# Cross attention: the products with V of four key tiles stand together, with eight buffers of probabilities

## The reference

```python
Q = (decoder_input @ W_q).reshape(B, Sd, HEADS, HEAD_DIM)      # B 4, Sd 1024, 16 heads of 32
K = (encoder_output @ W_k).reshape(B, Se, HEADS, HEAD_DIM)     # Se 2048
V = (encoder_output @ W_v).reshape(B, Se, HEADS, HEAD_DIM)
scores = jnp.einsum('bqhd,bkhd->bhqk', Q, K) / jnp.sqrt(jnp.float32(HEAD_DIM))
attn = jax.nn.softmax(scores, axis=-1)
out = jnp.einsum('bhqk,bkhd->bqhd', attn, V).reshape(B, Sd, E)
return out @ W_o + b_o
```

## Time and profile before

| | |
|---|---|
| median of 3 runs | 4630.41 us (4628.96 to 4638.13) |
| profiled execution | 4622.7 us |
| its span | 4621.0 us |
| TensorE (PE) busy | 4050.2 us, 88% |
| VectorE (DVE) busy | 2741.0 us, 59% |
| ScalarE (ACT) busy | 2096.2 us, 45% |
| GpSimd (POOL) busy | 2479.5 us, 54% |

### The profile page before, as it was taken

One profiled execution on the slowest core, in us unless ns is written; L12 is line 12 of the kernel. 1 busy time (PEld: TensorE's weight loads), 2 busy tenths in 40 slices (PEclk: granted clock), 3 DMA queues, 4 the chain that ended last, 5 costly groups with the idle time before them and its releaser, 6 DMA issues. The chain is left out here.

```text
span 4621.0 us, 61708 instructions
## 1 busy us (share of the span) xinstructions
PE 4050.2 (88%) x21906; PEld 2502.5 (54%) x21906; DVE 2741.0 (59%) x4978; ACT 2096.2 (45%) x3869; POOL 2479.5 (54%) x927
## 2 busy tenths in 40 slices
PE   6988999997779997999999999999999663339997
PEld 5874555554568884444444444444444342328885
DVE  4425777773443335777777777777776342316675
ACT  2112555553121110666666666666666322216665
POOL 0001333332000001999999999999999314527887
PEclk8996999998899996999999999999999875559999
DMA  4546454413555555122222222222220366524444
GB/s 146 173 163 127 97 112 95 94 47 128 187 200 171 176 170 135 25 61 64 62 65 56 56 58 56 56 56 56 56 56 6 128 204 97 97 59 74 81 81 64
DMA packets 283077, 449.71 MB, mean 97 GB/s; under 512 B 31384, under 2 KB 131736, under 8 KB 276632
## 3 DMA queue, kind: packets, MB, share of 16 engines
q1 hardware_dynamic: 259064, 407.26, 33.7%
q0 software_dynamic: 19776, 36.85, 4.8%
q10 hardware_dynamic: 3968, 2.10, 0.2%
HBM read 267.22 MB, written 178.91 MB: 97 GB/s over the span
## 5 line engine op out<-in xcount | busy, mean ns | idle before, releaser
L864 DVE TENSOR_REDUCE cross_neg_max<-cross_scores 128x1 f32<-128x512 f32 x2048 | 1265.6, 677 | 414.4 <-PE cross_scores L693 414.4
L653 POOL TENSOR_TENSOR cross_partial<-cross_partial,cross_probs 128x2048 f32<-128x2048 f32 x320 | 1465.6, 4580 | 66.7 <-ACT cross_probs L815 29.6
L815 ACT ACTIVATE cross_probs<-cross_shifted 128x512 f32<-128x512 f32 x2048 | 1074.3, 606 | 762.5 <-PE cross_shifted L705 728.2
L693 PE MATMUL cross_scores<-cross_k_stack,cross_q_stack 96*128 96x512 f32 x2048 | 876.2, 437 | 60.7 <-DMA cross_v<-v 33.1
L705 PE MATMUL cross_shifted<-cross_q_stack,cross_k_stack 98*128 98x512 f32 x2048 | 850.7, 420 | 11.5 <-ACT cross_probs L815 5.6
L705 PEld LDWEIGHTS cross_shifted<-cross_q_stack,cross_k_stack 98*128 98x128 f32 x2048 | 387.2, 190 | 382.7 <-issue 232.9
L693 PEld LDWEIGHTS cross_scores<-cross_k_stack,cross_q_stack 96*128 96x128 f32 x2048 | 395.3, 193 | 308.4 <-DVE cross_neg_max L864 224.3
L815 ACT ACTIVATE self_probs<-self_shifted 128x512 f32<-128x512 f32 (+3 forms) x768 | 358.7, 492 | 377.4 <-PE self_shifted L708 296.5
L864 DVE TENSOR_REDUCE self_neg_max<-self_scores 128x1 f32<-128x512 f32 (+3 forms) x768 | 388.3, 548 | 218.5 <-PE self_scores L693 109.2
L719 PE MATMUL cross_out<-cross_probs,cross_v 128*32 128x512 f32 x4096 | 494.2, 600 | 0.0
L693 PE MATMUL self_scores<-self_k_stack,self_q_stack 96*128 96x512 f32 (+3 forms) x768 | 308.4, 423 | 31.7 <-DMA self_v<-v 23.7
(11 more groups left out here) (249 smaller groups left out, 6282.4 us busy)
## 6 DMA issues: line engine op xcount, KB each, us to landing
cross_k_stack<-k_hi SPq DMA_DIRECT2D x32, 1024.0 KB, 19.0
self_q_stack<-q_hi SPq DMA_DIRECT2D x32, 512.0 KB, 6.9
self_k_stack<-k_hi SPq DMA_DIRECT2D x32, 512.0 KB, 15.6
out_a_in<-attn SPq DMA_DIRECT2D x16, 1024.0 KB, 9.5
x<-out_y SPq DMA_DIRECT2D x16, 1024.0 KB, 5.3
kv_x_in<-in_ctx SPq DMA_DIRECT2D x16, 1024.0 KB, 5.5
k_hi<-kv_out_hi SPq DMA_DIRECT2D x64, 256.0 KB, 2.6
k_lo<-kv_out_lo SPq DMA_DIRECT2D x64, 256.0 KB, 3.2
```

Source lines behind the costliest of these rows:

```text
L653: nc.gpsimd.tensor_tensor(total, total, own, ALU.add).then_inc(pool_added.sem, 1)
L693: mm = nc.tensor.matmul(scores[at][:, 0:width], q_st[0:96, w, h, q0:q0 + P], k_st[0:96, w, h, half * WIDE:half * WIDE + width], start=True ...
L815: nc.scalar.activation(probs[:, e % NE % PB, h, f:], shifted[n % SHIFTED][:, f:], ACT.Exp).then_inc(exped.sem, 1)
L864: nc.vector.tensor_reduce(neg_max[:, q % 2, column(a), half:half + 1], scores[n % (SLOTS * ROUNDS) % AHEAD][:, 0:width], AX.X, ALU.max, ne ...
```

## The change

The block of `values` comes every four steps (0, 4, 8 and 12 of a round) in place of every two, with the products of the four steps before it, and the ring of probabilities has eight buffers, not six. The self-attention keeps its values. The whole diff:

```diff
@@ -415,7 +415,8 @@
     LEAD = 18 if causal else 16
     QTILES = 8 if causal else 4
     COLS = 4 * QTILES
-    PB = 4 if causal else 6
+    PB = 4 if causal else 8
+    PV_BLOCK = 2 if causal else 4
     NPARTIAL = 1 if causal else 2
     SUM_LAG = 2 if causal else 4
     PARTS = 4 if causal else 8
@@ -740,7 +741,7 @@
 
             def block_of_values(it, e, begins):
 
-                for old in (e - 2, e - 1):
+                for old in range(e - PV_BLOCK, e):
                     if old >= 0 or not begins:
                         values(it, old)
 
@@ -761,7 +762,7 @@
                             score(it, n)
                         if h == 1 and e % 2:
                             block_of_sums(it, e, begins)
-                        elif h == 1:
+                        elif h == 1 and e % PV_BLOCK == 0:
                             block_of_values(it, e, begins)
                 if not more:
                     block_of_values(it, NE, False)
```

## The result

The changed kernel takes 4678.41 us (median of 4 runs, 4675.41 to 4684.86) against 4631.77 for the kernel before (4 runs, 4628.96 to 4638.13), a ratio of 1.0101, 95% interval 1.0083 to 1.0118: 47 us slower. The forecast was 4673, range 4656 to 4695. By the profiled executions it is 4676.6 against 4622.7, 53.9 more.

What follows compares the result with a forecast made beforehand. TensorE sets the pace, waiting for VectorE, which reads scores from three PSUM buffers. Rounds 2 to 30 add 43.8 us, round 31 2.9, less 0.8 (first round) and 1 (buffers): 45, taken as +43; median 4673, range 4656 to 4695.

Steps and rivals of the forecast that it cites:

- What bounds the kernel: Cross stage: TensorE sets the pace, but its long runs of scores wait for VectorE, at 0.60 us per score instead of 0.47.
- The formula: First to last of S scores, R reciprocals: 0.43 + 0.60 x (S - 4) + 0.40 x R + 0.74, if above 0.47 x (S - 1).
- The double block: Blocks of steps 0, 4, 8 and 12: 3.91 us to the first score taken, 4.24 with two blocks' full overhead.
- The third rival: Four-tile blocks have the upper overhead or hide a wait for the newest exponentials: 1.3 us more per round, 4712; chance 0.05.
- The sum: All stretches of a round together: 57.11 us against 55.60, 1.5 more per round, 43.8 over rounds 2 to 30.
- the load's time: Step 15: from loading the maxima back to the next round's first shifted matmul, 2.5 us, about what the transfer needs.
- The buffers: Eight buffers of probabilities instead of six end ScalarE's 14 waits for GpSimd at the wraps (26.3 us); gain taken as 1 us.
- Round 31 and the tail: Last VectorE-bound stretches end with step 9 of round 31, adding 2.9 us; from there GpSimd is the chain.
- The first round: Without reciprocals and sums of an older round, it gives 0.8 us back.
- this case: The forecast itself: +43 us, median 4673, own range 4664 to 4682; chance 0.73.
- a late write of the maxima: Step 14's write lands too late for step 15's load: 0.3 us per round gives 4682, up to 2 gives 4733; chance 0.12.

## Why the prediction came out right

**What bounds the kernel**: right. The formula of block, three buffers, 0.60 per maximum and 0.40 per reciprocal gives all seven stretches of the changed kernel to 0.03 us. What the prediction could not show, that it is VectorE and not the block itself that costs, is shown by the turned sign with halved maxima, by 13.70 us with four buffers, and by the gain of a block in every step.

**The double block**: right at its lower bound of 3.91. The third rival (1.3 more per round) is out.

**The sum**: 29 x 1.5 = 43.8 was predicted for the rounds, and 43.8 measured. This is partly luck: the typical round is 57.04, not 57.11, and other rounds make up for it. In the last round of each of the first seven passes step 12 to 0 takes 13.56 to 13.59 in place of 13.20. The trace says what for: the first weight load of the next round waits there for the reloaded maxima, here in one of them:

```profile
2065.33 0.19 PEld L706 LDWEIGHTS cross_shifted<-cross_q_stack,cross_k_stack 98*128 98x128 f32 x1 [0.69 <-DMA cross_q_stack<-cross_neg_dram]
```

That is 0.69 in each of the seven, against 0.3 at most in the other rounds but the last, and 0.38 x 7 = 2.7 us in all. The load is issued no later there (2062.25, 2.30 after the write), but the matmul comes 3.1 us behind it and not 2.6; why isn't shown. The prediction had only the write as a possible loss, and the load's time as just enough. The third round of each pass takes 9.19 in step 9 to 12 in place of 8.59, but the kernel before has the same 0.6 there.

**The buffers**: 1 us was allowed, and the run with them alone gave 0.8 in its rounds and nothing in the medians. ScalarE's waits were hidden, as argued, by a TensorE that had its own to wait for.

**Round 31 and the tail**: the place was right and the size not. Predicted was 2.9 up to step 9; from step 3 of the last but one round to the last sum it was 5.2 (107.4 against 102.2 before). The run with blocks of two at the end, 105.0, gives 2.8. The other 2.4 go with the clock's fall between the blocks of step 12 and step 0 (one trace with the closer blocks), of which the prediction had nothing, since it ended its account with step 9. "From there GpSimd is the chain" held only while the exponentials came in time.

**The first round**: 0.8 less was predicted. Step 3 of the second round came no earlier, at 1906.17 against 1906.21, but the stage itself had begun later: the first matmul for an exponential at 1842.54, before at 1841.23. From there to step 3 of the second round it took 63.6 us in place of 65.0.

**Outside the stage**: of the 53.9 us between the two profiled executions, 49.0 lie up to the stage's end (3674.75 against 3625.70) and 4.9 behind it, where nothing was changed. That part spans 995 to 1002 us over all the traces of this study, before's 995.3 being at the low end, so the 4.9 are not to be put down to the change; they may also be why the medians stand 47 apart and not 54. With the kernel before at 4631.77, the predicted 43 would have given 4675.

**The chances**: 0.73 for this case was not too much. The rival with most of the rest, a late write of the maxima, did not come true: the load is issued 2.29 us after the write, in the round shown and within 0.1 in all others but the last. ScalarE's queue in step 14 and 15:

```profile
3034.02 0.78 ACTq L841 DMA_DIRECT2D cross_neg_dram<-cross_neg_rows  x2
...
3036.31 0.63 ACTq L846 DMA_DIRECT2D cross_q_stack<-cross_neg_dram  x1
```

In this kernel the slowest write took 2.0 us to land and used up the slack, by the order of time: two of the loads come 2.37 and 2.38 after the write, the rest of them by 2.31. The 3.5 of the earlier trace rows did not come again, so what it would have cost isn't known.

## What to carry to other kernels

Batching work on one engine saves its change-overs and charges a neighbour that it feeds through only a few buffers: what the neighbour idles during the block is the block less what its buffers hold. Where the neighbour is slower per item than the batching engine, here 0.60 to 0.47, it never makes that up, and shorter blocks win although they cost more switches. When one neighbour's limit is lifted, the next is close: read the waits again, since its own small extra work (here the reciprocals) can keep it the limit. Before reordering, write the stretch as block + first item + pace x (items - buffers) + release, fit it to two rows of the trace, and then try it in both directions; the better change here was the opposite one.

## What was not expected of the hardware

The clock did not fall where TensorE waited for VectorE a thousand times (1.00 over 1731 us), but in the stage's last round, where the matmuls of the exponentials stood alone (1.00 up to 3608, 0.50 from 3609 to 3615, 1.00 again from 3616), and GpSimd stood 2.62 us for it later. Halving the maxima alone took 93 us off the kernel of before, 15 to 18 of them at the stage's start, and then met GpSimd's 53.04 us per round. With that gone too, the next limits were the maxima's way through DRAM (step 14 to 0, 6.9 in place of 6.05) and VectorE's reciprocals (1.06 for two halved maxima and one reciprocal, where TensorE needs 0.94): they all lie within 4 us of a round of 55.8.
